# Half-width mask pieces, one selector buffer and a third weight buffer in a macaron block on eight cores

## The chip, the cores and the metric

The kernel runs on all 8 cores of one Trainium2 chip. Each core does the same program on its own 1,024 of the 8,192 tokens and no core talks to another. The metric is device time in microseconds of the slowest core.

## What is computed

Three linear layers with residuals, each behind a layer norm over 4,096 features; the first and third have the same weights, given as 4-bit integers with a scale and a zero for each group of 128, and the second has a weight that is masked in blocks of 32 x 32:

```python
def attn(data, mask, weight, bias):          # weight (4096, 4096)
    bm = mask.reshape(Nb, 32, Kb, 32).sum(axis=(1, 3)) > 0
    wb = weight.reshape(Nb, 32, Kb, 32) * bm[:, None, :, None]
    return einsum('bsk,nk->bsn', data, wb.reshape(N, K)) + bias

def ffn(x, qweight, scales, scaled_zeros, bias):
    w = (qweight * scales + scaled_zeros).reshape(O, I)
    return einsum('bsi,oi->bso', x, w) + bias

x = x + 0.5 * ffn(layernorm(x), ...)
x = x + attn(layernorm(x), ...)
x = x + 0.5 * ffn(layernorm(x), ...)
```

## The kernel before

The residual R (8 token tiles of 128 x 4096, fp32) stays in SBUF. Each of the three sub-layers (sub 0, 1, 2) runs in two halves of four token tiles: layer norm and transposition into xnT, then 16 rounds (og) of 256 output columns. A round is four quarters q of 32 matmuls (line 623), each quarter with its own 512 KB slab of weights, one of three arena buffers; then a bias matmul (632) and two additions into R on VectorE (664).

Sub 0, half 0, called stage A here, also makes the weights. Between the quarters of a round it dequantises the quarters to come: qw rows are loaded by GpSimd's queue (322), VectorE builds diagonal scale matrices diag (341), TensorE multiplies (357, 362), ScalarE evicts into a slab (384), and SyncE writes the slab to DRAM scratch scr_f (391) for later. At the end of each round, emit_mask_work reads part of the mask: SyncE loads a piece into one of two mbuf buffers (409), VectorE sums it in groups of 32 columns into S1 (433), and for every 128 rows of the mask a matmul into psBM (446) sums over rows. A piece is 128 rows by 1,024 columns of int8; there are 128 pieces, 8 to a round, 2 of the first round's being taken earlier. A mask load waits for the reduction two pieces before.

After stage A comes a transposition for the next half (279, 292), and then emit_bm_finalize. It compares and transposes the 128 x 128 block mask and spreads its rows over the partitions: 32 steps, each a 32 KB selpad load on ScalarE's queue (487) into one of two selp2 buffers, a small matmul (499) and a copy into bmsel (508). A load waits for the matmul two steps before. This is the selection loop.

Sub 0, half 1, called stage B here, reads its slabs back from scr_f (595; quarters 0 and 2 on SyncE's queue, 1 and 3 on ScalarE's, since og * 4 + q is even or odd). Behind each round emit_attn_q puts nine chunks of the attention weight through: GpSimd's queue loads 128 x 1,024 elements from fp32 in DRAM to bf16 in a wtb buffer (525), VectorE expands the mask (538) and multiplies (542), SyncE writes the chunk to scratch scr_a (548). A load waits for the write of the chunk that had the slot before. There are 128 chunks: fourteen rounds with nine, one with two, one with none. Each engine and each queue works in program order: a round's nine writes stand on SyncE's queue ahead of the next round's slab loads, and its nine multiplications on VectorE behind the round's additions into R.

The rest of the program, sub 1 and sub 2, only reads slabs back and multiplies.

Of the kernel before, what the change touches and what calls it, by code (L numbers as in the profile page):

```python
# [38 lines left out]
def build_nc():  # L39
# [95 lines left out]
    wr_a_guard = [0, 0, 0]  # L135
    mult_done = {}
    m_load = {}
    m_red = [0] * 128
    s1_done = [0] * 32
    bm_mm = [0] * 32  # L140
    n_mask_emitted = [0]
# [257 lines left out]
    def emit_mask_load_one():  # L399
        blk = BLK()  # L400
        m = n_mask_emitted[0]
        nt, c = m // 4, m % 4
        slot = m % 2

        def f(eng, m=m, nt=nt, c=c, slot=slot):
            if m - 2 >= 0:
                W(eng, "s", eV, m_red[m - 2])
            q = sMb[slot]
            q.dma(eng.dma_start(out=mbuf[slot][:],
                                in_=mask[128 * nt:128 * (nt + 1),  # L410
                                         1024 * c:1024 * (c + 1)]))
            m_load[m] = (q, q.n)
        blk.sync(f)
        n_mask_emitted[0] += 1

    def emit_mask_work(nmax):
        blk = BLK()
        nmax = min(nmax, 128)
        while n_red_emitted[0] < nmax:
            while n_mask_emitted[0] < min(n_red_emitted[0] + 2, 128):  # L420
                emit_mask_load_one()
            m = n_red_emitted[0]
            nt, c = m // 4, m % 4
            slot = m % 2

            def f(v, m=m, nt=nt, c=c, slot=slot):
                q, val = m_load[m]
                W(v, "v", q, val)
                if nt >= 2 and c == 0:
                    W(v, "v", eT, bm_mm[nt - 2])  # L430
                with nc.allow_low_precision(
                        reason="mask 0/1 block sums <=32, exact in bf16"):
                    ins = v.tensor_reduce(  # L433
                        S1[nt % 2][:, 32 * c:32 * (c + 1)],
                        mbuf[slot].rearrange("p (a b) -> p a b", b=32),
                        axis=AX.X, op=ALU.add)
                m_red[m] = eV.inc(ins)
                if c == 3:
                    s1_done[nt] = eV.n
            blk.vector(f)  # L440

            if c == 3:
                def f_t(t_, nt=nt):
                    W(t_, "t", sCst, idn_load[0])
                    W(t_, "t", eV, s1_done[nt])
                    ins = t_.matmul(psBM[:, 0:128],  # L446
                                    nbsel_sb[:, 128 - 4 * nt:256 - 4 * nt],
                                    S1[nt % 2][:], start=(nt == 0), stop=(nt == 31))
                    bm_mm[nt] = eT.inc(ins)
                blk.tensor(f_t)  # L450
            n_red_emitted[0] += 1

    def emit_bm_finalize():
        blk = BLK()

        def f_v(v):
            W(v, "v", eT, bm_mm[31])
            eV.inc(v.tensor_single_scalar(bm_bf[:], psBM[:, 0:128], 0.0, ALU.is_gt))
        blk.vector(f_v)
        th = eV.n  # L460

        b0 = bank_seq[0] % 3
        bank_seq[0] += 1

        def f_t(t_, b0=b0, th=th):
            W(t_, "t", eV, th)
            W(t_, "t", dq_free[b0][0], dq_free[b0][1])
            bmtr[0] = eT.inc(t_.matmul(psDQ[:, 512 * b0:512 * b0 + 128],
                                       bm_bf[:], idn_sb[:], start=True, stop=True))
        blk.tensor(f_t)  # L470

        def f_ev(v, b0=b0):
            W(v, "v", eT, bmtr[0])
            dq_free[b0] = (eV, eV.inc(v.tensor_copy(bmT[:], psDQ[:, 512 * b0:512 * b0 + 128])))
        blk.vector(f_ev)
        bmT_done = eV.n

        for kt in range(32):
            pslot = kt % 2

            def f_ld(s, kt=kt, pslot=pslot):
                W(s, "a", eT, scope_guard.get("dq_all", 0))
                W(s, "a", eV, scope_guard.get("dq_allv", 0))
                W(s, "a", eV, scope_guard.get("mask_all", 0))
                if kt >= 2:
                    W(s, "a", eT, selp_mm[kt - 2])
                sSelp[pslot].dma(s.dma_start(out=selp2[pslot][:],
                                             in_=selpad_d[:, 128 * kt:128 * (kt + 1)]))
                selp_ld[kt] = sSelp[pslot].n
            blk.scalar(f_ld)  # L490

            b = bank_seq[0] % 3
            bank_seq[0] += 1

            def f_t(t_, kt=kt, pslot=pslot, b=b, bmT_done=bmT_done):
                W(t_, "t", sSelp[pslot], selp_ld[kt])
                W(t_, "t", eV, bmT_done)
                W(t_, "t", dq_free[b][0], dq_free[b][1])
                selp_mm[kt] = eT.inc(t_.matmul(psDQ[:, 512 * b:512 * b + 128],
                                               selp2[pslot][:], bmT[:],  # L500
                                               start=True, stop=True))
                selp_bank[kt] = b
            blk.tensor(f_t)

            def f_ev(v, kt=kt):
                b = selp_bank[kt]
                W(v, "v", eT, selp_mm[kt])
                dq_free[b] = (eV, eV.inc(v.tensor_copy(
                    bmsel_sb[:, 128 * kt:128 * (kt + 1)],
                    psDQ[:, 512 * b:512 * b + 128])))  # L510
            blk.vector(f_ev)
        bm_final[0] = eV.n

    def emit_attn_q(nmax):
        blk = BLK()
        while n_aq[0] < min(nmax, 128):
            ch = n_aq[0]
            og, hh = ch // 8, ch % 8
            wslot = ch % 2

            def f_gp(g, ch=ch, og=og, hh=hh, wslot=wslot):
                W(g, "g", eT, scope_guard.get("dq_all", 0))
                W(g, "g", eV, scope_guard.get("dq_allv", 0))
                W(g, "g", sWr_a[wslot], wr_a_guard[wslot])
                sWtb[wslot].dma(g.dma_start(  # L525
                    out=wtb[wslot][:],
                    in_=bass.AP(wt_t, og * 128 * 8192 + 1024 * hh,
                                [[8192, 128], [1, 1024]])))
                wtb_load[ch] = sWtb[wslot].n
            blk.gpsimd(f_gp)  # L530

            def f_v(v, ch=ch, og=og, hh=hh, wslot=wslot):
                W(v, "v", eV, bm_final[0])
                if ch >= 1:
                    W(v, "v", eV, mult_done[ch - 1])
                sel = bass.AP(bmsel_sb, 128 * 4 * hh + 8 * og,
                              [[4096, 128], [128, 4], [1, 8], [0, 32]])
                c = eV.inc(v.tensor_copy(
                    bexp[0].rearrange("p (a b c) -> p a b c", b=8, c=32), sel))
                W(v, "v", eV, c)  # L540
                W(v, "v", sWtb[wslot], wtb_load[ch])
                mult_done[ch] = eV.inc(v.tensor_tensor(  # L542
                    wtb[wslot][:], wtb[wslot][:], bexp[0][:], ALU.mult))
            blk.vector(f_v)

            def f_wr(s, ch=ch, og=og, hh=hh, wslot=wslot):
                W(s, "s", eV, mult_done[ch])
                sWr_a[wslot].dma(s.dma_start(
                    out=bass.AP(scr_a, og * 128 * 8192 + 1024 * hh,
                                [[8192, 128], [1, 1024]]),  # L550
                    in_=wtb[wslot][:]))
                wr_a[ch] = (wslot, sWr_a[wslot].n)
                wr_a_guard[wslot] = sWr_a[wslot].n
            blk.sync(f_wr)
            n_aq[0] += 1
# [116 lines left out]
    DQL = 2  # L672

    stM = ExitStack()
    mbuf = [stM.enter_context(nc.sbuf_tensor(f"mb{i}", [128, 1024], mybir.dt.int8)) for i in range(2)]

    with nc.Block() as blk:
        holder["blk"] = blk
# [24 lines left out]
        for og in range(16):  # L703
            emit_mm_round(0, 0, og, xnT_gate,
                          interleave=lambda q, og=og: emit_dq_quarter(
                              4 * og + q + 3, scl_ready))
            emit_mask_work(8 * (og + 1))
        scope_guard["dq_all"] = dq_mm[(15, 3, 1, 1)]
        scope_guard["dq_allv"] = eV.n
        stB.close()  # L710
        stM.close()
        stS = ExitStack()
        bmsel_sb = stS.enter_context(nc.sbuf_tensor("bmsel", [128, 4096], BF16))
        selp2 = [stS.enter_context(nc.sbuf_tensor(f"sp{i}", [128, 128], BF16))
                 for i in range(2)]
        stA = ExitStack()
        wtb = [stA.enter_context(nc.sbuf_tensor(f"wtb{i}", [128, 1024], BF16))
               for i in range(2)]
        bexp = [stA.enter_context(nc.sbuf_tensor("bexp0", [128, 1024], BF16))]

        emit_apply_transpose([4, 5, 6, 7], mm_done[(0, 0, 15)])
        xnT_gate = eV.n
        scope_guard["mask_all"] = m_red[127]
        emit_bm_finalize()

        next_c = [0] * 8
# [117 lines left out]
```

How the kernel before makes its waits and increments, by code:

```python
    def dma(self, instr):  # L28
        instr.then_inc(self.h, 16)
        self.n += 16
        return self.n
# [1 line left out]
    def inc(self, instr):  # L33
        instr.then_inc(self.h, 1)
        self.n += 1
        return self.n
# [66 lines left out]
    def W(eng, key, sem, val):  # L103
        if val is None or val <= 0:
            return
        k = (key, id(sem))
        if val > hwm.get(k, 0):
            eng.wait_ge(sem.h, val)
            hwm[k] = val
```

## Time and profile before

| | us |
|---|---|
| median of 3 runs (lowest to highest) | 3226.68 (3207.79 to 3280.79) |
| the profiled execution | 3216.21 |
| span of its slowest core (core 6) | 3214.6 |
| spans of the other cores | 3179.4 to 3214.5 |
| TensorE matmul busy, core 6 | 1806.2 (56% of the span) |
| VectorE busy | 885.3 (28%) |
| ScalarE busy | 679.1 (21%) |
| GpSimd busy | 204.7 (6%) |

The mean granted clock of TensorE is 0.785 to 0.788 on all cores. In the rows, times are microseconds from the start of the span; the arrow names what the engine waited for; SPq, ACTq and POOL rows with DMA_DIRECT2D are the issues of transfers, and their time runs from the first to the last issue merged in the row. PE is TensorE, DVE VectorE, ACT ScalarE, POOL GpSimd, SP SyncE.

### The profile page before, as it was taken

The numbers are of one execution on the slowest core, as the hardware profiler recorded it, in microseconds if no ns is written. First come the engines' busy times: TensorE is split into PE (matmuls) and PEld (weight loads), VectorE is DVE, ScalarE is ACT, GpSimd is POOL, SyncE is SP. The second block draws the span as 40 slices with busy tenths as digits, with TensorE's granted clock in tenths as the row PEclk, the third lists the DMA queues.
The fourth block names the chain that finished last, engine by engine and source line by source line (L and its number), as shares of the span: only waits on it lengthen the run. The fifth ranks groups of instructions, "written<-read, shape, count | busy, mean of one in ns | idle before, by whom it ended". The sixth has DMA issues, their size and how long they took to land.

```text
span 3214.6 us, 36817 instructions; the slowest of 8 cores (3179.4 to 3214.6 us)
## 1 busy us (share of the span) xinstructions
PE 1806.2 (56%) x14785; PEld 1435.7 (45%) x14785; DVE 885.3 (28%) x1348; ACT 679.1 (21%) x656; POOL 204.7 (6%) x392
## 2 busy tenths in 40 slices
PE   0155555464645342232242234599787959997986
PEld 0033333343423131131131223488666857885875
DVE  1534343433433412333322222200221231002000
ACT  0465646464645200000000000400300030003000
POOL 0011111111111000000000000000000000000000
PEclk9987777676867566566676567699798978997998
DMA  7123333233332144555545544155333424552575
GB/s 224 41 56 88 107 83 111 81 106 92 106 92 78 38 102 104 114 121 115 129 106 120 119 111 112 53 143 146 87 99 101 145 71 115 145 144 76 144 224 190
DMA packets 140870, 356.47 MB, mean 111 GB/s; under 512 B 23664, under 2 KB 40224, under 8 KB 138656
## 3 DMA queue, kind: packets, MB, share of 16 engines
q1 hardware_dynamic: 71280, 193.10, 18.5%
q0 software_dynamic: 41200, 67.68, 12.4%
q10 hardware_dynamic: 28224, 93.34, 10.1%
q8 instruction: 121, 1.98, 0.3%
q14 instruction: 45, 0.37, 0.0%
HBM read 304.27 MB, written 83.89 MB: 121 GB/s over the span
## 4 chain that ended last, share of the span: by engine, by line
PE 47%; DMA 24%; ACT 9%; DVE 9%; issue 7%; another core or an unknown queue 2%; SPq 0%; DVEq 0%; POOL 0%; ACTq 0%; POOLq 0%
PE psMM L623 42%; DMA wtb<-wt_t 8%; DMA mb<-mask 5%; DMA scr_a<-wtb 4%; ACT L384 4%; DMA slab<-scr_f 4%; DVE S L433 2%; ACT slab L384 2%; DVE stats L216 2%; PE psDQ L279 2%; ACT xnb L264 2%; DVE wtb L542 2%; PE psMM L632 2%; DMA qbf<-qw 1%
## 5 line engine op out<-in xcount | busy, mean ns | idle before, releaser
L623 PE MATMUL psMM<-slab,xnT 128*128 128x256 bf16 x12288 | 1479.0, 285 | 656.4 <-DMA slab<-scr_f 615.3
L623 PEld LDWEIGHTS psMM<-slab,xnT 128*128 128x128 bf16 x12288 | 1247.6, 102 | 869.9 <-issue 676.3
L664 DVE TENSOR_TENSOR R<-R,psMM 128x512 f32<-128x512 f32 x192 | 123.3, 684 | 1206.0 <-PE psMM L632 1206.0
L384 ACT ACT_TABLE_LOAD x256 | 328.4, 1283 | 385.2 <-PE psDQ L362 380.9
L245 ACT ACT_TABLE_LOAD x24 | 30.8, 1283 | 1314.4 <-DVE mv L238 1314.4
L341 DVE TENSOR_TENSOR diag<-idnh_sb,scl_sb 128x512 bf16<-128x512 bf16 x256 | 172.6, 691 | 347.9 <-PE psDQ L362 347.8
L357 PE MATMUL psDQ<-zrow,halfc 1*128 1x512 bf16 x256 | 100.2, 391 | 207.3 <-DVE diag L341 151.6
L433 DVE TENSOR_REDUCE S<-mb 128x32 bf16<-128x1024 int8 x128 | 152.6, 1216 | 180.7 <-DMA mb<-mask 180.5
L446 PE MATMUL psBM<-S,nbsel_sb 128*128 128x128 bf16 x32 | 8.5, 265 | 322.9 <-DVE S L433 322.9
L279 PE MATMUL psDQ<-idn_sb,xnb 128*128 128x128 bf16 x768 | 95.5, 303 | 164.2 <-ACT xnb L264 134.3
L264 ACT ACT_TABLE_LOAD x48 | 61.6, 1283 | 553.0 <-PE psMM L623 458.4
L542 DVE TENSOR_TENSOR wtb<-wtb,bexp 128x1024 bf16<-128x1024 bf16 x128 | 88.7, 693 | 301.4 <-DMA wtb<-wt_t 295.5
L279 PEld LDWEIGHTS psDQ<-idn_sb,xnb 128*128 128x128 bf16 x768 | 73.0, 136 | 186.4 <-issue 186.4
L384 ACT ACTIVATE slab<-psDQ 128x512 bf16<-128x512 f32 x256 | 152.9, 597 | 2.9
L292 DVE CAST xnT<-psDQ 128x512 bf16<-128x512 f32 x192 | 119.2, 684 | 115.6 <-PE psDQ L279 115.6
L446 PEld LDWEIGHTS psBM<-S,nbsel_sb 128*128 128x128 bf16 x32 | 3.3, 104 | 328.1 <-issue 328.1
L216 DVE BATCH_NORM_STATS2 stats<-R 128x6 f32<-128x512 f32 x192 | 116.3, 678 | 62.3 <-DMA R<-x_in 61.8
L357 PEld LDWEIGHTS psDQ<-zrow,halfc 1*128 1x128 bf16 x256 | 23.4, 91 | 243.6 <-issue 236.4
L525 POOL DMA_DIRECT2D wtb<-wt_t x128 | 68.2, 533 | 893.1 <-DMA scr_a<-wtb 829.5
L311 POOL DMA_DIRECT2D zrow<-zr x128 | 63.7, 497 | 858.9 <-PE psDQ L362 820.3
L362 PE MATMUL psDQ<-diag,qbf 128*128 128x128 bf16 x1024 | 105.4, 228 | 0.0
L264 ACT ACTIVATE xnb<-R,nmi,istd 128x2048 bf16<-128x2048 f32 x48 | 100.5, 2093 | 0.6
(29 smaller groups left out, 357.0 us busy)
## 6 DMA issues: line engine op xcount, KB each, us to landing
slab<-scr_f SPq DMA_DIRECT2D x96, 512.0 KB, 4.5
slab<-scr_f ACTq DMA_DIRECT2D x96, 512.0 KB, 4.4
qbf<-qw POOLq DMA_DIRECT2D x128, 256.0 KB, 3.8
scr_f<-slab SPq DMA_DIRECT2D x64, 512.0 KB, 3.1
wtb<-wt_t POOLq DMA_DIRECT2D x128, 256.0 KB, 4.8
scr_a<-wtb SPq DMA_DIRECT2D x128, 256.0 KB, 2.3
slab<-scr_a SPq DMA_DIRECT2D x64, 512.0 KB, 4.1
slab<-scr_a ACTq DMA_DIRECT2D x64, 512.0 KB, 4.5
```

Of the source, the lines that this page charges most:

```text
L216: eV.inc(v.bn_stats(stats6[:, lane + 6 * c: lane + 6 * c + 6], bass.AP(R, t * D + 512 * c, [[8 * D, 128], [1, 512]])))
L264: apply_done[t] = eA.inc(s.activation(xb[:], bass.AP(R, t * D + 2048 * kh, [[8 * D, 128], [1, 2048]]), AF.Identity, scale=istd[:, t:t + 1] ...
L279: ins = t_.matmul(psDQ[:, 512 * b + 128 * j:512 * b + 128 * (j + 1)], xb[:, 128 * (4 * kq + j):128 * (4 * kq + j + 1)], idn_sb[:], start=T ...
L292: dq_free[b] = (eV, eV.inc(v.tensor_copy(dst, src)))
L341: diag_ready[dslot] = (eV, eV.inc(v.tensor_tensor(dst, in0, in1, ALU.mult)))
L357: t_.matmul(psDQ[:, 512 * b:512 * (b + 1)], halfc[:], zrow[zslot][0:1, 512 * h:512 * (h + 1)], start=True, stop=False)
L362: ins = t_.matmul(psDQ[:, 512 * b + 128 * j:512 * b + 128 * (j + 1)], qbf[qslot][:, 512 * h + 128 * j:512 * h + 128 * (j + 1)], diag4[dslo ...
L384: dq_free[b] = (eA, eA.inc(s.activation(dst, srcp, AF.Identity)))
L433: ins = v.tensor_reduce(S1[nt % 2][:, 32 * c:32 * (c + 1)], mbuf[slot].rearrange("p (a b) -> p a b", b=32), axis=AX.X, op=ALU.add)
L542: mult_done[ch] = eV.inc(v.tensor_tensor(wtb[wslot][:], wtb[wslot][:], bexp[0][:], ALU.mult))
L623: ins = t_.matmul(psMM[:, 1024 * pg + 256 * tb:1024 * pg + 256 * (tb + 1)], xnT[:, 512 * kt + 128 * tb:512 * kt + 128 * (tb + 1)], arena[s ...
L664: eV.inc(v.tensor_tensor(dst, dst, src, ALU.add))
```

## The change

The mask is read in 256 pieces of 128 x 512 and no longer in 128 pieces of 128 x 1,024: eight to a row tile, 16 to a round (2 of the first round's earlier). Buffers stay two. The selector has one buffer: each of the 32 loads waits for the matmul of the step before. The weight chunks rotate over three buffers, not two, with the semaphores that exist already.

```diff
 def emit_mask_load_one():
-        nt, c = m // 4, m % 4
+        nt, c = m // 8, m % 8
         slot = m % 2
...
             q.dma(eng.dma_start(out=mbuf[slot][:],
                                 in_=mask[128 * nt:128 * (nt + 1),
-                                         1024 * c:1024 * (c + 1)]))
+                                         512 * c:512 * (c + 1)]))
...
 def emit_mask_work(nmax):
-        nmax = min(nmax, 128)
+        nmax = min(nmax, 256)
         while n_red_emitted[0] < nmax:
-            while n_mask_emitted[0] < min(n_red_emitted[0] + 2, 128):
+            while n_mask_emitted[0] < min(n_red_emitted[0] + 2, 256):
...
                     ins = v.tensor_reduce(
-                        S1[nt % 2][:, 32 * c:32 * (c + 1)],
+                        S1[nt % 2][:, 16 * c:16 * (c + 1)],
                         mbuf[slot].rearrange("p (a b) -> p a b", b=32),
...
-            if c == 3:
+            if c == 7:
                 def f_t(t_, nt=nt):
...
         for kt in range(32):
-            pslot = kt % 2
+            pslot = 0
...
-                if kt >= 2:
-                    W(s, "a", eT, selp_mm[kt - 2])
+                if kt >= 1:
+                    W(s, "a", eT, selp_mm[kt - 1])
...
 def emit_attn_q(nmax):
-            wslot = ch % 2
+            wslot = ch % 3
...
-    mbuf = [... f"mb{i}", [128, 1024], mybir.dt.int8)) for i in range(2)]
+    mbuf = [... f"mb{i}", [128, 512], mybir.dt.int8)) for i in range(2)]
...
-            emit_mask_work(8 * (og + 1))
+            emit_mask_work(16 * (og + 1))
...
-        selp2 = [... f"sp{i}", [128, 128], BF16)) for i in range(2)]
+        selp2 = [... "sp0", [128, 128], BF16))]
         stA = ExitStack()
         wtb = [stA.enter_context(nc.sbuf_tensor(f"wtb{i}", [128, 1024], BF16))
-               for i in range(2)]
+               for i in range(3)]
```

## Rows read from the trace of the kernel before

**Rows 1.** The page's chain that ended last, shares of the span by line.
```profile
PE psMM L623 42%; DMA wtb<-wt_t 8%; DMA mb<-mask 5%; DMA scr_a<-wtb 4%; ACT L384 4%; DMA slab<-scr_f 4%; DVE S L433 2%; ACT slab L384 2%; DVE stats L216 2%; PE psDQ L279 2%; ACT xnb L264 2%; DVE wtb L542 2%; PE psMM L632 2%; DMA qbf<-qw 1%
```

**Rows 2.** Stretches: length, busy PE, PEld, DVE, ACT, POOL, granted clock, DMA share, GB/s.
```profile
10.00:60.00 50.00, 0.00 (x0) 0.00 (x0) 0.00 (x0) 0.00 (x0) 0.00 (x0) 1.00 1.00 313
...
192.00:1055.30 863.30, 467.04 (x3364) 311.39 (x3364) 332.03 (x404) 462.16 (x490) 125.79 (x240) 0.75 0.34 94
...
1093.00:1131.00 38.00, 8.61 (x35) 3.66 (x36) 9.21 (x33) 0.00 (x0) 0.00 (x0) 0.50 0.15 36
1130.60:1987.00 856.40, 250.84 (x1982) 206.00 (x1981) 235.01 (x363) 5.94 (x8) 67.17 (x126) 0.64 0.51 115
```

**Rows 3.** Timeline of one mask block: start, duration, engine, line, tiles, count, wait.
```profile
674.21 13.61 SPq L409 DMA_DIRECT2D mb<-mask  x8
678.09 2.35 DVE L433 TENSOR_REDUCE S<-mb 128x32 bf16<-128x1024 int8 x2 [8.35 <-DMA mb<-mask]
681.59 2.35 DVE L433 TENSOR_REDUCE S<-mb 128x32 bf16<-128x1024 int8 x2 [1.15 <-DMA mb<-mask]
...
688.54 1.22 DVE L433 TENSOR_REDUCE S<-mb 128x32 bf16<-128x1024 int8 x1 [1.13 <-DMA mb<-mask]
...
689.97 5.46 PE L623 MATMUL psMM<-slab,xnT 128*128 128x256 bf16 x32
```

**Rows 4.** Groups by line and shape: count, busy us, mean ns, idle before.
```profile
L433 DVE TENSOR_REDUCE S<-mb 128x32 bf16<-128x1024 int8 x128 | 152.6, 1216 | 180.7 <-DMA mb<-mask 180.5
L664 DVE TENSOR_TENSOR R<-R,psMM 128x512 f32<-128x512 f32 x192 | 123.3, 684 | 1206.0 <-PE psMM L632 1206.0
```

**Rows 5.** DMA issues by line: count, size of one, median us to landing.
```profile
mb<-mask SPq DMA_DIRECT2D x128, 128.0 KB, 2.1
...
sp<-selpad ACTq DMA_DIRECT2D x32, 32.0 KB, 1.8
```

**Rows 6.** Timeline of the selection loop: steps 1 and 2, 3, 5 and 32.
```profile
1093.23 0.39 PE L499 MATMUL psDQ<-bmT,sp 128*128 128x128 bf16 x2 [0.54 <-DVE bmT L474]
...
1095.39 0.26 PE L499 MATMUL psDQ<-bmT,sp 128*128 128x128 bf16 x1 [1.77 <-DMA sp<-selpad]
...
1097.70 0.27 PE L499 MATMUL psDQ<-bmT,sp 128*128 128x128 bf16 x1 [1.27 <-DMA sp<-selpad]
...
1130.46 0.27 PE L499 MATMUL psDQ<-bmT,sp 128*128 128x128 bf16 x1 [0.38 <-DMA sp<-selpad]
```

**Rows 7.** Timeline of stage B: most of its first chunk block, ends of its last.
```profile
1149.07 0.69 DVE L542 TENSOR_TENSOR wtb<-wtb,bexp 128x1024 bf16<-128x1024 bf16 x1 [0.17 <-DVE bexp L538]
...
1152.36 0.53 POOL L525 DMA_DIRECT2D wtb<-wt_t  x1 [95.66 <-DMA scr_a<-wtb]
1154.15 0.53 POOL L525 DMA_DIRECT2D wtb<-wt_t  x1 [1.25 <-DMA scr_a<-wtb]
1156.92 0.69 DVE L542 TENSOR_TENSOR wtb<-wtb,bexp 128x1024 bf16<-128x1024 bf16 x1 [4.70 <-DMA wtb<-wt_t]
1159.21 0.69 DVE L542 TENSOR_TENSOR wtb<-wtb,bexp 128x1024 bf16<-128x1024 bf16 x1 [0.81 <-DMA wtb<-wt_t]
...
1183.09 0.69 DVE L542 TENSOR_TENSOR wtb<-wtb,bexp 128x1024 bf16<-128x1024 bf16 x1 [5.89 <-DMA wtb<-wt_t]
1184.33 0.83 SPq L595 DMA_DIRECT2D slab<-scr_f  x2
...
1190.52 16.51 PE L623 MATMUL psMM<-slab,xnT 128*128 128x256 bf16 x128 [43.62 <-DMA slab<-scr_f]
...
1919.59 0.69 DVE L542 TENSOR_TENSOR wtb<-wtb,bexp 128x1024 bf16<-128x1024 bf16 x1 [0.17 <-DVE bexp L538]
...
1952.80 0.69 DVE L542 TENSOR_TENSOR wtb<-wtb,bexp 128x1024 bf16<-128x1024 bf16 x1 [3.85 <-DMA wtb<-wt_t]
```

**Rows 8.** DMA queues from 1212 to 1246 us (8 chunk loads): packets, MB, share of 16 engines.
```profile
q0 software_dynamic: 1149, 2.09, 44.9%
q1 hardware_dynamic: 1019, 1.84, 14.1%
```

More of the change, by code:

```diff
@@ L137, in build_nc @@
     m_load = {}
-    m_red = [0] * 128
+    m_red = [0] * 256
     s1_done = [0] * 32
@@ L417, in emit_mask_work @@
         blk = BLK()
-        nmax = min(nmax, 128)
+        nmax = min(nmax, 256)
         while n_red_emitted[0] < nmax:
-            while n_mask_emitted[0] < min(n_red_emitted[0] + 2, 128):
+            while n_mask_emitted[0] < min(n_red_emitted[0] + 2, 256):
                 emit_mask_load_one()
             m = n_red_emitted[0]
-            nt, c = m // 4, m % 4
+            nt, c = m // 8, m % 8
             slot = m % 2
@@ L437, in f @@
                 m_red[m] = eV.inc(ins)
-                if c == 3:
+                if c == 7:
                     s1_done[nt] = eV.n
             blk.vector(f)
-            if c == 3:
+            if c == 7:
                 def f_t(t_, nt=nt):
@@ L674, in build_nc @@
     stM = ExitStack()
-    mbuf = [stM.enter_context(nc.sbuf_tensor(f"mb{i}", [128, 1024], mybir.dt.int8)) for i in range(2)]
+    mbuf = [stM.enter_context(nc.sbuf_tensor(f"mb{i}", [128, 512], mybir.dt.int8)) for i in range(2)]
     with nc.Block() as blk:
@@ L713, in build_nc @@
         bmsel_sb = stS.enter_context(nc.sbuf_tensor("bmsel", [128, 4096], BF16))
-        selp2 = [stS.enter_context(nc.sbuf_tensor(f"sp{i}", [128, 128], BF16))
-                 for i in range(2)]
+        selp2 = [stS.enter_context(nc.sbuf_tensor("sp0", [128, 128], BF16))]
         stA = ExitStack()
         wtb = [stA.enter_context(nc.sbuf_tensor(f"wtb{i}", [128, 1024], BF16))
-               for i in range(2)]
+               for i in range(3)]
         bexp = [stA.enter_context(nc.sbuf_tensor("bexp0", [128, 1024], BF16))]
@@ L722, in build_nc @@
         xnT_gate = eV.n
-        scope_guard["mask_all"] = m_red[127]
+        scope_guard["mask_all"] = m_red[255]
         emit_bm_finalize()
```

## Prediction

> **What bounds the kernel now.** I read the page's chain of work first, to see which kinds of wait set the end, then the busy times by stage, then the timeline inside one repeat of each stage that the change touches. The chain puts 42% on the large matmuls; beside them it holds three waits that the change touches: the weight chunk's load (wtb, 8%) and write (scr_a, 4%), the mask load (5%) and the mask reduction (2%) [rows 1]. So no single engine is the bound. The stages show it: TensorE is busy 467 us of 863 in stage A (first sub-layer, first token half, with dequantisation and mask work), 9 of 38 in the selection loop, and 251 of 856 in stage B (second half, with the weight chunks) [rows 2]. A microsecond added to or taken from a serial wait in these three stretches moves the end by about a microsecond.
>
> Stage A ends each of its 16 rounds with a mask block. VectorE reduces one piece that was loaded ahead, then waits until SyncE has passed the four scr_f writes, then takes the pieces as they come; TensorE starts the next round's 32 matmuls only 0.2 us after the last reduction ends (688.54 + 1.22, then 689.97) [rows 3]. Nothing of the next round runs beside the block. In stage B each round's nine chunks run between the R additions and the next round's slab load. The slab's load stands behind the nine writes on SyncE's queue (1184.33, 1.2 us after the ninth multiplication starts), and TensorE starts at 1190.52, after 43.62 us of waiting [rows 7].
>
> **Mask pieces: 128 become 256, each half as wide.** Two slots are kept. One slot's cycle is a reduction plus its reload: pairs start at 678.09, 681.59 and so on, and the block's last piece at 688.54, so three cycles take 10.45 us, 3.48 each [rows 3]. Less the reduction's 1.22 that leaves 2.26 us for release, issue and landing of 128 KB. For 64 KB there is no row. The 32 KB selpad load, in the same kind of loop, has a slot cycle of 2.31 us (1095.39 to 1097.70), less 0.27 for the matmul: 2.04 [rows 6]; the landing times say the same, 2.1 against 1.8 us [rows 5]. In a line between the two, 64 KB takes 2.11 us. The reduction itself: 1,024 elements take 1,216 ns; half is 608 and a 512-element VectorE pass takes 684 ns [rows 4]; I take 0.68. The new slot cycle is then 2.79 us: the piece is halved, the cycle falls by only a fifth. After its first, preloaded piece a block has 7 left now, three cycles and one reduction: 3 x 3.48 + 1.22 = 11.7 us. Afterwards 15 are left: 7 x 2.79 + 0.68 = 20.2 us, which is 8.5 more. The first block has only 6 of 8 pieces now and 14 of 16 later, so 2 against 6 cycles after the preloaded one: 17.4 - 8.2 = 9.2 more. Sum: 15 x 8.5 + 9.2 = **+137 us**. Bounds: 0.61 and 2.04 give 7 x 2.65 + 0.61 = 19.2, or +121 in all; 0.68 and 2.26 give 21.3, or +154. VectorE's diag products, queued behind the block, and SyncE's next scr_f write move with it; ScalarE and the qw loads idle beside it already, so no cover is lost.
>
> The row says that a half-size load saves 0.15 us of 2.26. The Trainium skill ("DMA: Bandwidth & Descriptors", on the anatomy of one DMA) says that a DMA costs a fixed 2.0 us plus its bytes over 436 GB/s, and that transfers should be batched. By that the 64 KB load saves 0.15 us too, and it speaks against this part: the mask sum by it would be the same 137 us.
>
> **Selection loop: two selpad slots become one.** 32 small matmuls each need a load. With two slots 31 steps take 1130.46 - 1093.23 = 37.2 us [rows 6]. With one slot a step is the whole cycle, load after matmul, 2.31 us: 31 x 2.31 = 71.6, **+34 us**. Bounds: by the bare landing time 1.8 + 0.27 = 2.07 a step, +27; by twice the present mean step, 2.40, +37. TensorE's first matmul of stage B stands behind this loop in program order, so all of it counts. ScalarE's slab load q1 stands behind the same loads and is needed only after the q0 matmuls.
>
> **Weight chunks: two wtb slots become three.** A chunk's slot is multiplied, written out, then reloaded. From the first to the ninth multiplication of a block it takes 34.0 us in the first of fourteen full blocks and 33.2 in the last [rows 7]; the mean of the fourteen is 33.3, four slot cycles of 8.3. With three slots the ninth chunk is the third of the third group: two cycles and two spacings within a group. The spacing is that of two landings in one pair, 1156.92 to 1159.21, 2.3 us. The cycle grows, since a third load shares the DMA engines: the second load of a pair takes 5.1 us from its issue (1154.15 to 1159.21) where the first takes 4.6 (1152.36 to 1156.92), so a further one costs about 0.5 again. 2 x 8.8 + 2 x 2.3 = 22.2 us, 11.1 saved. After it the slab load meets three reloads and not two; I give it 0.5 us of the present 6.2 (1184.33 to 1190.52). Net 10.6 x 14 = **-148 us**. The short block with two chunks and the round without any gain nothing. Bounds: with the shortest cycle shown, 7.85 (1149.07 to 1156.92), 2 x 7.85 + 4.6 = 20.3, 13 x 14 = -182; with a cycle longer by the third load's whole engine time, 44.9% of 34 us over 8 loads = 1.9 us [rows 8], 2 x 10.2 + 4.6 = 25.0, 8.3 a block less 0.5, -109.
>
> **Sum.** 137 + 34 - 148 = +23 us on the profiled execution's own 3216.2 us: 3239, against the three runs' median of 3226.7, which lies 10 us above the profiled one. The matmul clock I leave as it is: the granted clock is 0.75 over stage A, 0.64 over stage B and 0.50 (the 1.2 GHz level) in the selection loop [rows 2], and after the change TensorE still pauses before every one of these rounds, some 33 us where it was 43.6 in stage B [rows 7], and longer in stage A.
>
> **Rivals.**
> - *The DMA engines fill up and the third slot brings little (slower).* The chunk phase keeps them 59% busy, 44.9 and 14.1 by queue [rows 8]; that is 0.59 x 34 / 8 = 2.5 us of engine time a chunk, and the plan asks for a chunk each 22.2 / 8 = 2.8. All cores read at once at full share in the input stage, 313 GB/s [rows 2], and a chunk reads 512 KB of fp32 and writes 256 KB: 786 KB / 313 = 2.5 us. Close to the plan, not beyond it. If the block shrinks by 5 us only, the sum is 171 - 70 = +101, 3317 us. It ends over +2% (3291) where a block saves less than about 7 us. The Trainium skill ("HBM Reference", specifications) gives each core of a busy pair about 358 GB/s; that would be 2.2 us a chunk and speaks against this rival, and no row here reaches that rate.
> - *Half a piece costs half (faster).* If both loads in flight and the reduction scale with size, the cycle is 1.74 us and a block grows by 7 x 1.74 + 0.61 - 11.7 = 1.1: 18 us in all, 3216 + 18 + 34 - 148 = 3120. For it: loads overlap. Against it: the 32 KB and 128 KB landings, 1.8 and 2.1 us, a quarter of the size for six sevenths of the time [rows 5].
> - *The smaller pieces are covered.* If TensorE had work during a mask block, the +137 would be hidden and the time 3102. Its start right behind the last reduction speaks against that [rows 3].
>
> **How the numbers follow.** Forecast of a near draw: 0.75. Full DMA engines: 0.14. Halving or cover: 0.11 together. The ends of the three sums give 3216 + 121 + 27 - 182 = 3182 and 3216 + 154 + 37 - 109 = 3298. All terms at their worst at once is unlikely, but part of the slow rival lies just there: 3180 to 3295 should hold it 8 times in 10. This kernel's measurement tells about 2% from no change, that is below 3162 and above 3291. Faster 0.09, same 0.78, slower 0.13, where some of both rivals falls inside.
>
> **What would show it.** Stage A about 137 us longer, with 256 reductions of some 0.68 us and pairs 2.8 us apart; the selpad slot cycle unchanged, 32 matmuls over some 72 us; stage B about 148 us shorter, TensorE's wait for scr_f slabs down from 43 to 33 us a round, DMA share in a chunk phase from 0.59 to 0.8 or more. It is wrong if mask pairs come under 2.4 us apart, or if the ninth chunk starts later than 26 us after the first.

## The result and the profile after

The changed kernel takes 3283.45 us (median of 9 runs) against 3222.79 (median of 10). The ratio is 1.0186 with a 95% interval of 1.0159 to 1.0212. In part of the runs of either kernel the cores of one die or of both show a lower granted clock and take some per cent longer; all ratios here compare the other runs. The profiled execution took 3280.48 us; core 3, the slowest, spans 3278.9. That is inside the range and 41 us above the predicted 3239. It is slower, but the interval reaches past 1.02, so whether it is the 2% that the prediction calls slower stays open. The near draw came, but two of its terms were off beyond their own bounds, and in part offset each other.

Cut at the same four events on the slowest core of each profile, in us: stage A runs from the first slab matmul to the last psBM matmul, stage B from its first slab matmul to the first one of sub-layer 1.

| | stage A | transposition | selection loop | stage B | rest of the span |
|---|---|---|---|---|---|
| before (core 6) | 862.3 | 38.0 | 37.4 | 928.1 | 1348.8 |
| after (core 3) | 971.8 | 38.0 | 72.4 | 848.2 | 1348.5 |
| difference | +109.5 | 0 | +35.0 | -79.9 | -0.3 |
| predicted | +137 | 0 | +34 | -148 | 0 |

The page's chain of work, shares by line, where the mask load went from 5% to 8%, the chunk load from 8% to 4%, and the selector load came in [rows 1]:

```profile
PE psMM L623 41%; DMA mb<-mask 8%; DMA slab<-scr_f 5%; DMA wtb<-wt_t 4%; ACT L384 4%; DMA scr_a<-wtb 4%; DVE S L433 3%; ACT slab L384 2%; DVE stats L216 2%; PE psDQ L279 2%; ACT xnb L264 2%; DMA sp<-selpad 2%; DVE wtb L542 2%; PE psMM L632 1%
```

**Stage A.** The timeline of one mask block, and the reduction's row of the groups by line (count, busy us, mean ns, idle before):

```profile
538.64 21.34 SPq L409 DMA_DIRECT2D mb<-mask  x16
542.01 1.28 DVE L433 TENSOR_REDUCE S<-mb 128x16 bf16<-128x512 int8 x2 [8.45 <-DMA mb<-mask]
544.72 1.29 DVE L433 TENSOR_REDUCE S<-mb 128x16 bf16<-128x512 int8 x2 [1.43 <-DMA mb<-mask]
...
560.85 0.69 DVE L433 TENSOR_REDUCE S<-mb 128x16 bf16<-128x512 int8 x1 [1.27 <-DMA mb<-mask]
...
561.75 4.50 PE L623 MATMUL psMM<-slab,xnT 128*128 128x256 bf16 x23
```

```profile
L433 DVE TENSOR_REDUCE S<-mb 128x16 bf16<-128x512 int8 x256 | 170.8, 684 | 280.8 <-DMA mb<-mask 279.4
```

The pairs are 2.7 us apart (542.01, 544.72) where they were 3.5, and the piece takes 684 ns where it took 1,216. A block runs from 542.01 to 560.85 + 0.69, 19.5 us, where the one shown of before takes 11.7 [rows 3]. TensorE still starts its next 32 matmuls at once behind it (561.75).

**Selection loop.** TensorE's timeline: steps 1, 2 and 32, with one matmul every 2.2 to 2.3 us, each behind its own load, and stage B right after the last [rows 6]:

```profile
1200.96 0.26 PE L499 MATMUL psDQ<-bmT,sp 128*128 128x128 bf16 x1 [0.55 <-DVE bmT L474]
...
1203.12 0.27 PE L499 MATMUL psDQ<-bmT,sp 128*128 128x128 bf16 x1 [1.89 <-DMA sp<-selpad]
...
1273.24 0.27 PE L499 MATMUL psDQ<-bmT,sp 128*128 128x128 bf16 x1 [2.23 <-DMA sp<-selpad]
...
1273.37 16.80 PE L623 MATMUL psMM<-slab,xnT 128*128 128x256 bf16 x128
```

**Stage B.** The timeline of the first block of chunks. It shows the first, third, fourth, sixth and ninth multiplication (line 542), the reload of the third chunk's buffer (525), the slab load and TensorE's start [rows 7]:

```profile
1292.87 0.69 DVE L542 TENSOR_TENSOR wtb<-wtb,bexp 128x1024 bf16<-128x1024 bf16 x1 [0.17 <-DVE bexp L538]
...
1296.20 0.69 DVE L542 TENSOR_TENSOR wtb<-wtb,bexp 128x1024 bf16<-128x1024 bf16 x1 [0.17 <-DVE bexp L538]
...
1300.72 0.69 DVE L542 TENSOR_TENSOR wtb<-wtb,bexp 128x1024 bf16<-128x1024 bf16 x1 [3.03 <-DMA wtb<-wt_t]
...
1301.84 0.53 POOL L525 DMA_DIRECT2D wtb<-wt_t  x1 [3.50 <-DMA scr_a<-wtb]
...
1306.19 0.69 DVE L542 TENSOR_TENSOR wtb<-wtb,bexp 128x1024 bf16<-128x1024 bf16 x1 [1.55 <-DMA wtb<-wt_t]
...
1317.05 0.69 DVE L542 TENSOR_TENSOR wtb<-wtb,bexp 128x1024 bf16<-128x1024 bf16 x1 [2.96 <-DMA wtb<-wt_t]
1318.28 0.99 SPq L595 DMA_DIRECT2D slab<-scr_f  x2
...
1325.78 16.21 PE L623 MATMUL psMM<-slab,xnT 128*128 128x256 bf16 x128 [35.08 <-DMA slab<-scr_f]
```

The ninth multiplication starts 24.2 us after the first (34.0 before); over the fourteen blocks 25.1 against 33.3 in the mean. The first three chunks lie ready and are multiplied 1.7 us apart; the ninth then stands two slot cycles behind the third, 10.0 and 10.9 us here (1296.20, 1306.19, 1317.05). TensorE's wait is 35.1 us where it was 43.6. Stretches of the changed kernel (length, busy PE, PEld, DVE, ACT, POOL, granted clock, DMA share, GB/s), a chunk block and the two stages [rows 2]:

```profile
1293.00:1317.00 24.00, 0.00 (x0) 0.00 (x0) 10.97 (x16) 0.00 (x0) 3.70 (x7) 0.50 0.73 153
191.00:1163.00 972.00, 460.56 (x3364) 308.66 (x3364) 350.64 (x531) 462.11 (x490) 125.99 (x240) 0.72 0.32 84
1273.40:2050.00 776.60, 254.84 (x1982) 207.98 (x1982) 234.97 (x363) 5.94 (x8) 68.07 (x125) 0.65 0.59 127
```

The DMA engines' share in a chunk block rose from 0.59 [rows 8] to 0.73. The landing times beside it: DMA issues inside stage B by line (count, size, median us to landing), first of before, then of the changed kernel:

```profile
scr_a<-wtb SPq DMA_DIRECT2D x126, 256.0 KB, 2.3
wtb<-wt_t POOLq DMA_DIRECT2D x126, 256.0 KB, 4.9
slab<-scr_f SPq DMA_DIRECT2D x28, 512.0 KB, 6.1
```

```profile
scr_a<-wtb SPq DMA_DIRECT2D x126, 256.0 KB, 3.1
wtb<-wt_t POOLq DMA_DIRECT2D x124, 256.0 KB, 5.5
slab<-scr_f SPq DMA_DIRECT2D x26, 512.0 KB, 9.1
```

The write of a chunk lands 0.8 us later than before, its load 0.6 later, and SyncE's slab load 3 us later.

### The profile page after: what moved, and what is told of

Its sections match the earlier page's. It is cut to its first block, busy times and chain, and to the rows that moved or that the text cites. A ratio compares the mean times of both kernels' runs of the same rounds, so it can differ in the third digit from the quotient of the medians.

```text
span 3278.9 us, 37329 instructions; the slowest of 8 cores (3233.2 to 3278.9 us)
## 1 busy us (share of the span) xinstructions
PE 1803.0 (55%) x14785; PEld 1434.5 (44%) x14785; DVE 903.6 (28%) x1476; ACT 679.0 (21%) x656; POOL 206.4 (6%) x392
## 4 chain that ended last, share of the span: by engine, by line
PE 47%; DMA 24%; DVE 10%; ACT 9%; issue 7%; another core or an unknown queue 2%; SPq 0%; DVEq 0%; ACTq 0%; POOL 0%; POOLq 0%
PE psMM L623 41%; DMA mb<-mask 8%; DMA slab<-scr_f 5%; DMA wtb<-wt_t 4%; ACT L384 4%; DMA scr_a<-wtb 4%; DVE S L433 3%; ACT slab L384 2%; DVE stats L216 2%; PE psDQ L279 2%; ACT xnb L264 2%; DMA sp<-selpad 2%; DVE wtb L542 2%; PE psMM L632 1%
## 5 line engine op out<-in xcount | busy, mean ns | idle before, releaser
L433 DVE TENSOR_REDUCE S<-mb 128x16 bf16<-128x512 int8 x256 | 170.8, 684 | 280.8 <-DMA mb<-mask 279.4
```

What stands on the lines that cost most here:

```text
L433: ins = v.tensor_reduce(S1[nt % 2][:, 16 * c:16 * (c + 1)], mbuf[slot].rearrange("p (a b) -> p a b", b=32), axis=AX.X, op=ALU.add)
```

## The experiments

Stage lengths of every kernel run, from its profile, in us:

| | span | stage A | selection | stage B |
|---|---|---|---|---|
| before | 3214.6 | 862.3 | 37.4 | 928.1 |
| after | 3278.9 | 971.8 | 72.4 | 848.2 |
| e1 third chunk buffer alone | 3134.2 | 856.8 | 37.0 | 848.2 |
| e2 mask pieces alone | 3351.1 | 982.2 | 36.3 | 939.7 |
| e3 one selector buffer alone | 3256.7 | 860.1 | 74.1 | 934.0 |
| e4 after, four mask buffers | 3147.3 | 825.6 | 72.8 | 836.4 |
| e5 after, slab loads on ScalarE | 3138.5 | 983.4 | 74.1 | 694.7 |
| e7 before, slab loads on ScalarE | 3075.6 | 855.8 | 41.2 | 790.2 |
| e8 after, half chunk loads | 3200.7 | 972.0 | 72.3 | 762.6 |
| e9 before, half chunk loads | 3134.5 | 864.7 | 36.7 | 841.2 |
| e6 after, stage B side by side | 3072.3 | 976.2 | 73.6 | 631.0 |
| e10 all together | 3055.0 | 1012.6 | 18.8 | 640.1 |
| e11 quarter mask pieces | 3595.8 | 1247.1 | 36.8 | 929.2 |
| e12 all, two waits taken out | 2620.9 | 585.7 | 19.0 | 635.0 |

Kernels that share a stage's code show how far one profile may be trusted. Stage A took 855.8 to 864.7 us in the five kernels with 128 pieces and 971.8 to 983.4 in the five with 256 in two buffers, +117 between the means. The selection loop took 36.3 to 37.4 us in five of the six kernels with two buffers (41.2 in e7, whose first slab load of stage B stands behind the selector's loads) and 72.3 to 74.1 in six with one, +36. Stage B took 928.1 to 939.7 us in the four with two chunk buffers (before, e2, e3, e11) and 836.4 to 848.2 in the three with three (after, e1, e4), -88. Together that is +65, where the two profiles above give +64.

### One part at a time (e1, e2, e3)

e1 is the kernel before with a third chunk buffer. It keeps the second selector buffer by laying it in a tile that is free by then, for lack of room:

```diff
+                W(s, "a", eT, bm_mm[31])
...
-            wslot = ch % 2
+            wslot = ch % 3
...
-        selp2 = [... f"sp{i}" ... for i in range(2)]
+        selp2 = [... "sp0" ..., S1[0]]
...
-               for i in range(2)]     # wtb
+               for i in range(3)]
```

> The kernel before with three weight-chunk buffers and nothing else; the second selpad buffer lies in the S1 tile, which is free by then, since the third chunk buffer leaves no room for it. Theory (contention of the transfers gives part of the gain back): stage B is 80 us shorter, as in the changed kernel: ninth multiplication 25 us after the first (33.3 before), SyncE's slab load to TensorE's start 7.8 us (5.9 before). The rest stays: about 3137 us, ratio 0.975. Rival (the loss in the chunk stage comes from a different start, the mask pieces or the single selector buffer before it): the full 148 us, about 3070.

Measured: ratio 0.9751 (0.9668 to 0.9834), 80 us less. Stage B is 848.2 us, as in the changed kernel; ninth multiplication after 25.3 us, slab load to TensorE's start 7.3 us. The full 148 us can't be had even without the other parts, so the shortfall lies in the chunk stage itself.

e2 is the change without its last two parts, so the edit is on the changed kernel:

```diff
-            pslot = 0
+            pslot = kt % 2
...
-            wslot = ch % 3
+            wslot = ch % 2
...
```

> The kernel before with 256 half-width mask pieces and nothing else. Theory (a piece costs mostly its fixed latency): stage A 109 us longer as in the changed kernel, pairs 2.7 us apart, about 3326 us, ratio 1.034. Rival (part of the block is covered and shows only because of other changes): under 50 us longer.

Measured: ratio 1.0415 (1.0361 to 1.0470), 116 to 151 us more. Stage A is 120 us longer where 109 were expected; another 12 us are in stage B, which the edit doesn't touch, so they are a difference between cores and executions.

e3, on the kernel before:

```diff
-            pslot = kt % 2
+            pslot = 0
...
-                if kt >= 2:
-                    W(s, "a", eT, selp_mm[kt - 2])
+                if kt >= 1:
+                    W(s, "a", eT, selp_mm[kt - 1])
```

> The kernel before with one selpad buffer and nothing else. Theory: 32 steps of 2.26 us in a row, 72 us where it was 37, all on the path: +35 us, ratio 1.011. Rival (part of the loop is hidden behind stage B's first slab load): under 15 us. The three parts alone should add up to the whole change, +64 us, if they don't act on each other.

Measured: ratio 1.0117 (1.0075 to 1.0158); the loop takes 74.1 us, 36.7 more, and the ratio's 38 us say that all of it is on the path. The three parts add to -80 + 134 + 38 = +92 us, the whole change measured +60. The half-widths of the three intervals, 27, 18 and 13 us, make 35 together (root of the sum of squares), so this doesn't show that the parts act on each other.

### What a mask piece costs (e4, e11)

e4, on the changed kernel:

```diff
-        slot = m % 2
+        slot = m % 4
...
-            if m - 2 >= 0:
-                W(eng, "s", eV, m_red[m - 2])
+            if m - 4 >= 0:
+                W(eng, "s", eV, m_red[m - 4])
...
-            while n_mask_emitted[0] < min(n_red_emitted[0] + 2, 256):
+            while n_mask_emitted[0] < min(n_red_emitted[0] + 4, 256):
...
-    mbuf = [... [128, 512], mybir.dt.int8)) for i in range(2)]
+    mbuf = [... [128, 512], mybir.dt.int8)) for i in range(4)]
```

> The changed kernel with four mask buffers of half width, loads four pieces ahead: the bytes of the kernel before. Theory (the loss is the reload's latency, about 2.0 us whatever the size, seen once for every two pieces): with four in flight VectorE's 0.69 us a piece sets the pace, and three pieces lie ready at the start: a block takes 13 x 0.69 = 9 us after its first landing where the changed kernel takes 19.7 and the kernel before 11.7; stage A falls by some 160 us, total about 3120, ratio 0.97. Rival (256 transfers are too many for SyncE's queue or the DMA engines): the block stays above 14 us and the total above 3190.

Measured: ratio 0.9729 (0.9673 to 0.9785) against the kernel before. Its timeline, same columns:

```profile
445.22 1.86 DVE L433 TENSOR_REDUCE S<-mb 128x16 bf16<-128x512 int8 x3
...
450.90 13.30 SPq L409 DMA_DIRECT2D mb<-mask  x16
455.06 2.46 DVE L433 TENSOR_REDUCE S<-mb 128x16 bf16<-128x512 int8 x4 [7.98 <-DMA mb<-mask]
457.94 4.12 DVE L433 TENSOR_REDUCE S<-mb 128x16 bf16<-128x512 int8 x6 [0.41 <-DMA mb<-mask]
...
464.60 5.65 PE L623 MATMUL psMM<-slab,xnT 128*128 128x256 bf16 x26
```

After the wait the reductions run nearly end to end: 9.5 us from 455.06 to TensorE's start, for 13 pieces, as forecast. Stage A is 825.6 us, 146 less than with two buffers. The number of transfers is the same; only how many are in flight differs. (Stage B was 12 us shorter on that core and the rest of its span 26 longer than in the changed kernel, so this span fell by 132; the two ratios are 147 us apart.)

e11, on the kernel before, halves the piece twice:

```diff
-        nt, c = m // 4, m % 4
+        nt, c = m // 16, m % 16
...
-                                         1024 * c:1024 * (c + 1)]))
+                                         256 * c:256 * (c + 1)]))
```

> The kernel before with 512 mask pieces of 256 columns, two buffers. Theory (a fixed part of about 1.9 us and a small part by size): a slot cycle of 0.42 + 1.95 = 2.4 us, against 2.7 at 512 columns and 3.5 at 1,024; a block holds 31 pieces after the first, 15 cycles and one reduction, 36 us where the kernel before has 11.7: total about 3216 + 16 x 24.5 = 3608. Rival (cost by size): the cycle halves again to 1.35 and the block stays near 20 us, total near 3350.

Measured: 3597.4 us, the forecast 3608. Timeline of two pairs, and the load's landing row (count, size, us):

```profile
546.72 0.74 DVE L433 TENSOR_REDUCE S<-mb 128x8 bf16<-128x256 int8 x2 [9.54 <-DMA mb<-mask]
549.02 0.90 DVE L433 TENSOR_REDUCE S<-mb 128x8 bf16<-128x256 int8 x2 [1.56 <-DMA mb<-mask]
```

```profile
mb<-mask SPq DMA_DIRECT2D x512, 32.0 KB, 1.8
```

The same row of the changed kernel, with the selector's:

```profile
mb<-mask SPq DMA_DIRECT2D x256, 64.0 KB, 1.9
...
sp<-selpad ACTq DMA_DIRECT2D x32, 32.0 KB, 1.7
```

So three sizes have been measured, 128, 64 and 32 KB: 2.1, 1.9 and 1.8 us to landing [rows 5], and slot cycles of 3.48, 2.71 and 2.34 us (medians). Less the reduction (1.22, 0.69, 0.42) that leaves 2.26, 2.02 and 1.92: a quarter of the size takes 0.34 us off a wait of 2.26.

### What the third chunk buffer meets (e8, e9)

The same edit on the changed kernel (from chunk 3) and on the kernel before (from chunk 2). Both leave the second half of each later chunk unloaded, so they multiply old weights there and serve for timing alone:

```diff
-                    out=wtb[wslot][:],
+                    out=wtb[wslot][:, 0:(1024 if ch < 3 else 512)],
...
-                                [[8192, 128], [1, 1024]])))
+                                [[8192, 128], [1, 1024 if ch < 3 else 512]])))
```

> The changed kernel; from the fourth chunk on only the first half of each chunk is loaded, so half of the weights used are stale. It halves the bytes of the chunk loads and nothing else. Theory (with three in flight the block waits for the DMA engines, 1.9 us of engine time a load): the block from first to ninth multiplication falls from 25.1 to about 19 us and the slab's wait from 7.8 to about 6.3. Rival (latency that does not depend on size): the block stays above 23.

> The kernel before with the same half loads, from the third chunk on, half of the weights used stale. Theory: with two in flight each slot's cycle of 8.3 us falls only by its own load's half, 0.95 us, and a little overlap: the block falls from 33.3 to about 29, which is less than with three buffers. Rival (size matters equally little or much): both blocks fall by the same share.

Measured: the block falls from 25.1 to 21.0 us with three buffers and from 33.3 to 27.6 with two, by 16 and 17%. The expected split, 19 against 29, didn't come, nor did the rival for three buffers, a block above 23; the rival for two, the same share in both, did. The slab's wait falls from 7.8 to 6.4 us with three buffers and from 5.9 to 5.2 with two. DMA issues inside stage B, e8 and then e9:

```profile
scr_a<-wtb SPq DMA_DIRECT2D x108, 256.0 KB, 2.7
wtb<-wt_t POOLq DMA_DIRECT2D x108, 128.0 KB, 4.3
```

```profile
scr_a<-wtb SPq DMA_DIRECT2D x95, 256.0 KB, 2.0
...
wtb<-wt_t POOLq DMA_DIRECT2D x93, 128.0 KB, 3.1
```

At equal bytes a half load lands in 4.3 us with three slots in use and in 3.1 with two, and the write in 2.7 and 2.0. Halving the bytes helps, so bytes in the engines are part of the delay; but the third load in flight costs 1.2 us of landing even at half size. For the loads these runs don't separate the engines' share from the order within GpSimd's queue. The writes are on SyncE's queue, and there the engines' share goes with the delay. In the changed kernel's first block the first chunk's write took 2.0 us to land and the third's 4.3; the DMA share (last but one column) in these two stretches:

```profile
1293.60:1295.60 2.00, 0.00 (x0) 0.00 (x0) 1.66 (x3) 0.00 (x0) 0.00 (x0) 0.50 0.34 131
1297.00:1301.30 4.30, 0.00 (x0) 0.00 (x0) 1.27 (x2) 0.00 (x0) 0.53 (x1) 0.50 0.91 147
```

The share is the time that packets took, and the rate rose far less, from 131 to 147 GB/s. Whether the packets wait for the engines or for something behind them, with all eight cores at work, no run here tells.

### Whether the block must be on the path at all (e5, e7, e6)

e5 on the changed kernel and e7 on the kernel before, one edit, which puts all slab loads of stage B on ScalarE's queue:

```diff
             key = "s" if par == 0 else "a"
+            if sub == 0:
+                key = "a"
```

> The changed kernel with all slab loads of stage B on ScalarE's queue, so that none stands behind the chunk writes on SyncE's. Theory (the chunk block is on the path only because the next round's slab load queues behind its writes): TensorE's 16 us and the block run side by side, a round takes the block plus the additions, about 31 us with more contention, where it took 54: 14 x 23 = 320 us less, about 2960 us. Rival (VectorE's order binds them anyway, or the DMA engines are full): a round stays above 45 us and less than 130 us is saved.

> The kernel before with the same move of the slab loads and still two chunk buffers. Theory: a round takes the two-buffer block of 33.3 us and the additions, about 36 where it took 58.6: 14 x 22 = 310 us less, about 2910 us; the third buffer is then worth less than in the kernel as it was, since slab loads share the DMA engines with the block. Rival as for the other: less than 130 us.

Measured: 3142.5 and 3077.1 us, medians of 4 and 5 runs without an interval, so I go by stage B: 153 and 138 us shorter, half of what was expected and just more than the rival allows. The third buffer was expected to be worth less beside the moved loads; between e7's stage B and e5's lie 96 us, where the two profiles without the move have 80. Two things in e5's trace hold it up. First the end of one of rounds 2 to 5, then, from another stretch, three starts of TensorE later on:

```profile
1525.90 1.28 ACT L245 ACT_TABLE_LOAD   x1 [55.67 <-DVE mv L238]
1526.01 1.58 ACTq L597 DMA_DIRECT2D slab<-scr_f  x3
...
1531.49 16.88 PE L625 MATMUL psMM<-slab,xnT 128*128 128x256 bf16 x128 [40.70 <-DMA slab<-scr_f]
```

```profile
1696.62 12.75 PE L625 MATMUL psMM<-slab,xnT 128*128 128x256 bf16 x96 [29.97 <-DVE R L666]
...
1731.26 12.51 PE L625 MATMUL psMM<-slab,xnT 128*128 128x256 bf16 x96 [12.02 <-DVE R L666]
...
1773.76 13.42 PE L625 MATMUL psMM<-slab,xnT 128*128 128x256 bf16 x96 [25.37 <-DVE R L666]
```

In rounds 2 to 5 the slab loads now stand behind istd on ScalarE, the inverse standard deviation for the next layer norm. It needs statistics that VectorE makes behind the round's chunks; ScalarE had been idle for 55.67 us when it came, and these four rounds take 57 to 98 us. The move took the loads off one queue and behind an instruction of another. In the later rounds TensorE does run beside the chunks, the two shown take 34.6 and 42.5 us, and TensorE then waits for the additions into R, which stand behind the chunks on VectorE. The DMA share there is 0.85:

```profile
1731.00:1769.00 38.00, 16.70 (x132) 13.63 (x132) 11.69 (x17) 0.00 (x0) 4.75 (x9) 0.72 0.85 177
```

e6 writes the order anew on the changed kernel: chunks ahead of the round's own additions, the next round's slab loads ahead of the last three chunk writes, all on SyncE:

```diff
-            emit_mm_round(0, 1, og, xnT_gate)
-            emit_attn_q(9 * (og + 1))
+            emit_mm_round(0, 1, og, xnT_gate,
+                          interleave=lambda q, og=og: emit_attn_q(
+                              9 * og + (4, 4, 4, 6)[q]))
...
+        if stage_b:
+            if og < 15:
+                nxt = [(slab_rr[0] + q) % 3 for q in range(4)]
+                for q in range(3):
+                    load_q(q, og + 1, nxt)
+            emit_attn_q(9 * (og + 1))
```

> The changed kernel with stage B's order written anew: a round's chunks stand on VectorE ahead of its own R additions, so they run beside its 128 matmuls; SyncE issues the next round's slab loads q0 to q2 before the last three chunk writes, and all slab loads of the stage are on SyncE, none behind ScalarE's istd, which held them up in rounds 2 to 5 when they were on ScalarE. Theory (DMA engines are the bound once nothing is serial): a round asks for 9 x 2.5 us of chunk transfers and about 7 us of slab loads, so 33 to 36 us where it takes 53.4: stage B from 848 to about 590 us, total about 3020. Rival (order on VectorE, not the transfers): a round stays above 42 us, as with the loads on ScalarE.

Measured: ratio 0.9592 (0.9384 to 0.9800); stage B 631 us against 590 forecast and 848 in the changed kernel. Two stretches of it, columns as above; the DMA share is 0.77 and 0.81 where stage B as a whole had 0.59. The rounds with nine chunks take 35 to 43 us, where 33 to 36 were forecast. That the transfers set this pace is not shown: the share reached 0.92 from 1610 to 1648 us of e5.

```profile
1600.00:1680.00 80.00, 33.14 (x264) 27.13 (x264) 32.13 (x49) 0.00 (x0) 10.28 (x18) 0.71 0.77 168
1300.00:1380.00 80.00, 39.41 (x297) 31.10 (x297) 29.10 (x43) 0.00 (x0) 10.90 (x20) 0.73 0.81 186
```

### A version that beats both (e10, e12)

e10 joins e6 and e4, gives the selector four buffers, and spreads the mask over the quarters:

```diff
-                          interleave=lambda q, og=og: emit_dq_quarter(
-                              4 * og + q + 3, scl_ready))
-            emit_mask_work(16 * (og + 1))
+                          interleave=lambda q, og=og: (
+                              emit_dq_quarter(4 * og + q + 3, scl_ready),
+                              emit_mask_work(16 * og + 4 * (q + 1))))
```

> The same stage B; in stage A the mask work is spread, four half-width pieces after each dequantised quarter, with four mask buffers; the selection loop has four selector buffers (the free S1 tiles and idnh). Theory (a mask block costs what it holds up, not what it computes): VectorE has 2.8 us of reductions beside ScalarE's 7.6 us of eviction a quarter, so the pieces disappear: stage A from 972 to about 600 us; the selection loop from 72 to about 35; total about 2620. Rival (SyncE's mask loads wait behind each quarter's scr_f write, so each quarter waits some 4 us for them): stage A above 750, total above 2770.

Measured: ratio 0.9524 (0.9452 to 0.9595). The selection loop fell to 18.8 us (35 forecast), but stage A rose to 1012.6: the rival. A stretch of its timeline:

```profile
506.16 1.86 DVE L433 TENSOR_REDUCE S<-mb 128x16 bf16<-128x512 int8 x3
...
512.20 0.33 SPq L391 DMA_DIRECT2D scr_f<-slab  x1
512.62 2.23 SPq L409 DMA_DIRECT2D mb<-mask  x4
515.31 0.69 DVE L433 TENSOR_REDUCE S<-mb 128x16 bf16<-128x512 int8 x1 [7.29 <-DMA mb<-mask]
...
516.21 5.01 PE L627 MATMUL psMM<-slab,xnT 128*128 128x256 bf16 x32
```

Three pieces lie ready, the fourth is issued behind the quarter's scr_f write (512.20, then 512.62) and lands at 515.3; VectorE stands 7.3 us for one piece, with the R additions and the diag products behind it, and TensorE stands as well (516.21). One late 64 KB load a quarter, four times a round, costs more than the whole block at the round's end did: stage A is 187 us longer than in e4, which has the same four buffers.

e12 takes out that wait, and TensorE's for the S1 sums, whose matmul is now issued behind the next quarter's 32. Its edit against e10:

```diff
-                blk.tensor(f_t)
+                bm_pending.append(f_t)
...
+        while n_mask_emitted[0] < min(n_red_emitted[0] + 4, 256):
+            emit_mask_load_one()
```

> The kernel with everything again, with the two waits taken out that its trace shows: SyncE issues the next quarter's four mask loads before the quarter's scr_f write (in the trace the fourth piece came 8.6 us late, behind that write), and the matmul over rows, psBM, is issued after the next quarter's 32 matmuls. Theory: the mask pieces now lie beside ScalarE's 7.6 us of eviction a quarter, so stage A falls from 1013 to about 620 us, total about 2680. Rival (TensorE and ScalarE alternate, as the quarters outside the mask blocks do now, at 8 to 9 us a quarter and more with the pieces between): stage A 700 to 800, total 2750 to 2850.

Measured: 2628.7 us, ratio 0.8185 (0.8123 to 0.8248). Stage A takes 585.7 us (620 forecast), 386 fewer than in the changed kernel, for the same instructions. How the gain is shared between the two waits is not shown, since both went at once. A stretch that is almost all of stage A, columns as above:

```profile
191.00:790.00 599.00, 474.07 (x3412) 316.44 (x3412) 341.52 (x544) 469.47 (x495) 127.61 (x243) 0.86 0.60 139
```

In stage A TensorE is now busy 474 of 599 us where it was 461 of 972, and ScalarE 469 of 599. Of ScalarE's 469 us only 146 are evictions of 0.60 us; 313 are table loads of 1.28 us, one ahead of each eviction, in this kernel as in all the others, and no run here took them out. The granted clock rose to 0.86 there from 0.72, and over the execution from 0.78 to 0.86.

## Why the prediction was right, and where it wasn't

**The bound.** That stages A, selection and B are serial chains in which a wait moves the end one for one was right: the selector buffer alone made its loop 36.7 us longer and the kernel 38 (e3), the chunk buffer alone made stage B and the kernel 80 us shorter (e1), and the rest of the span stayed within 0.3 us between these two profiles.

**The mask term, +137, measured +109.5 (+120 in e2, +117 between the means).** Its mechanism was right, its size too high, below even the lower bound of 121. The cycle was put at 2.79 us and is 2.71, so a block grew by 7.9 us and not 8.5. The time from the R additions to the first landing became 0.6 shorter, which the sum didn't have; the thirteen middle rounds grew by 7.1 us each (54.7 to 61.8). The first round grew by 7.1, the fifteenth by 5.0 and the last by 4.6, where the sum had 9.2, 8.5 and 8.5. The choice of 2.11 us for the 64 KB wait, on the line between 32 and 128 KB, was close: 2.02. The Trainium skill's fit ("DMA: Bandwidth & Descriptors", the anatomy of one DMA, there for transfers that GpSimd issues: 2.0 us plus bytes over 436 GB/s) gives as an estimate 0.15 us between 128 and 64 KB and 0.08 between 64 and 32; the runs show 0.24 and 0.10 in the cycles, 0.2 and 0.1 in the landings. A large fixed part and a small one by size hold here too; the landings themselves, 1.8 to 2.1 us, lie 0.2 to 0.3 below the fit.

**The selection term, +34, measured +35 (+36 between the means).** Right, by the row of the two-buffer loop, since each of its slots was already a chain of its own.

**The chunk term, -148, measured -80 (-88 between the means).** This step failed in size, beyond the -109 that the prediction gave as its bad end. A block was to take two cycles of 8.8 us and two spacings of 2.3, 22.2 us. It takes two cycles of 10.9 and two spacings of 1.7, 25.1 us: the spacings are those of chunks that lie ready, and the cycle is longer than the 10.2 of the bad end. The prediction added 0.5 us to the cycle for the third load and nothing for the write. In the traces, over the fourteen blocks and along the slots that end in the ninth chunk, a load lands in 5.2 us where it took 4.4, and a write in 4.2 where it took 2.5. So the larger part of the extra 2.6 us is the write, a term that was put at nothing. Each block gives 8.1 us and not 11.1. And the slab load behind the block, which I let grow by 0.5 us, grew by 2.0 (5.9 to 7.8). TensorE's start to the next block's first multiplication adds 0.3. Together 14 x (8.1 - 2.0 - 0.3) = 81. The error was to read contention off the second load of a pair alone and not off every transfer that is under way at the same time: the write and the slab load were in the rows too.

**The rivals.** The full DMA engines came true in part. The share in a chunk block went to 0.73, not to the 0.8 forecast, with single writes at 0.91. The block saved 5.8 us net of the slab, between the 5 that this rival put at 3317 us and the 7 at which it decides. With the other two terms as forecast the total would have been 3216 + 171 - 81 = 3306, above the range. That it came out inside is in part luck: the mask term was too high by 27 us, and two errors of opposite sign, 68 and 27 us, left one of 41. Halving and cover are out: pairs are 2.7 us apart, not under 2.4, and TensorE starts right behind the block.

**The clock.** 0.72 in stage A (0.75 before) and 0.65 in stage B (0.64), 0.50, the lower level of 1.2 GHz, in a chunk block, in which TensorE does nothing. Leaving it out cost little: in the stretches shown TensorE's busy time is 461 us where it was 467 in stage A, and 255 where it was 251 in stage B.

## What to carry to other kernels

Count, for a loop of load, use and reload, how many loads are in flight against the landing time, which for 32 to 128 KB was 1.8 to 2.1 us here: halving a piece at two buffers cost 110 us, and the same half pieces at four buffers took 146 off that, 37 less than the kernel before. When a buffer is added to a loop of transfers, lengthen every transfer of the loop and the one that follows it, not just the added one. Before sizing the buffers of a serial block, ask which queue puts it on the path: here moving the same work beside the matmuls gave more than any buffer, 217 us in stage B (e6) against 80, and in stage A together with the buffers 386 (e12) against 146. Both took two tries, since one late load in an engine's order stops all that stands behind it.

## What the runs showed of the hardware

A 256 KB chunk write landed in 2.3 us (median) with two chunk loads in flight and in 3.1 with three, at a DMA share of 0.59 and 0.73 over the block. Within one block of the changed kernel it was 2.0 us while the share was 0.34 and 4.3 while it was 0.91, so a mean share well below one hides stretches in which the engines are nearly full. A chunk load of half the bytes took 3.1 us with two in flight and 4.3 with three. Share is not bytes: the chunk loads, which convert fp32 to bf16, moved 2.09 MB in 44.9% of the engines' time, the other queue 1.84 MB in 14.1% [rows 8]. The highest share read over 38 us of stage B was 0.92, in e5; over the 50 us of the input stage it was 1.00, at 313 GB/s [rows 2].
